# A selective-scan block on one core: three shared PSUM banks for products, one Silu for four chunks, decays computed ahead in SBUF, and B times u for two states in one instruction

## What is computed

```
xn = layer_norm(x); xs, z = split(xn @ in_w)            # 512 channels each
xc = silu(causal_conv4(xs) + conv_b)
delta = softplus(xc @ xd_w @ dtp_w + dtp_b)
Bm = xc @ xB_w;  Cm = xc @ xC_w                         # 16 states each
dA = exp(delta * A);  dBx = (delta * xc) * Bm
h_t = dA_t * h_(t-1) + dBx_t;   y_t = sum over n of h_t * C_t      # for each of 16 states
out = ((y + D * xc) * silu(z)) @ out_w + x
```

## Time and profile before

| what | us |
|---|---|
| median of 3 runs | 11806.0 |
| lowest and highest | 11800.15, 11808.89 |
| the profiled execution | 11784.14 |
| its span, first to last instruction | 11782.3 |
| busy: TensorE, VectorE, ScalarE, GpSimd | 9023.3, 9032.0, 5977.4, 7664.1 |
| mean granted TensorE clock | 0.829 |

### The profile page before, as it was taken

How to read it: one execution, slowest core, us unless ns; L and a number is a source line. 1 busy time by engine, 2 the same in 40 slices (tenths; PEclk the granted TensorE clock), 3 DMA queues, 4 the chain that set the end, 5 groups by cost and what they waited for, 6 DMA issues and landing times. The chain is left out here.

```text
span 11782.3 us, 151965 instructions
## 1 busy us (share of the span) xinstructions
PE 9023.3 (77%) x42776; PEld 7086.5 (60%) x42776; DVE 9032.0 (77%) x13553; ACT 5977.4 (51%) x8945; POOL 7664.1 (65%) x7270
## 2 busy tenths in 40 slices
PE   6777777777777777777777777777777777799998
PEld 5656555555556555655565555556565655577776
DVE  5888888888888888888888888888888888333332
ACT  4555555555555555555555555555555555244443
POOL 5777777777777777777777777777777778100000
PEclk7878787888888788888788878888888787799999
DMA  2221122222211222222211222122211221000000
GB/s 80 76 68 63 63 78 72 76 70 71 76 65 57 73 78 72 78 68 76 71 64 58 78 72 78 68 71 76 68 64 62 78 72 66 22 11 11 11 11 9
DMA packets 366106, 730.08 MB, mean 62 GB/s; under 512 B 143670, under 2 KB 188890, under 8 KB 365274
## 3 DMA queue, kind: packets, MB, share of 16 engines
q1 hardware_dynamic: 361560, 717.54, 18.3%
q10 hardware_dynamic: 3714, 2.89, 0.1%
HBM read 699.27 MB, written 21.05 MB: 61 GB/s over the span
## 5 line engine op out<-in xcount | busy, mean ns | idle before, releaser
L443 POOL TENSOR_TENSOR bu<-b_all,u_buf 128x514 f32<-128x514 f32 x4096 | 5100.3, 1269 | 156.6 <-DVE ch L837 150.9
L654 ACT ACTIVATE decay<-delta,neg_a 128x512 f32<-128x512 f32 x4096 | 2805.9, 689 | 3436.8 <-DVE h_ps L837 2248.6
L1080 PE MATMUL y_ps<-ident,ch 128*128 128x128 f32 x16384 | 2940.2, 322 | 1747.3 <-DVE ch L855 851.4
L1080 PEld LDWEIGHTS y_ps<-ident,ch 128*128 128x128 f32 x16384 | 2193.9, 164 | 2571.3 <-DVE ch L855 1339.9
L837 DVE TENSOR_TENSOR_SCAN ch<-decay,bu 128x256 f32<-128x256 f32 x4096 | 2908.6, 730 | 778.1 <-ACT decay L654 766.3
L837 DVE TENSOR_TENSOR_SCAN h_ps<-decay,bu 128x256 f32<-128x256 f32 x4096 | 2836.4, 736 | 273.2 <-POOL bu L443 120.3
L452 POOL TENSOR_TENSOR ch<-ch,c_all 128x512 f32<-128x512 f32 x1024 | 1345.5, 1314 | 1974.1 <-DVE ch L837 1973.6
L966 PE MATMUL w_ps<-xn,in_w 128*128 128x257 f32 x4096 | 1235.3, 457 | 280.6 <-ACT xn L559 151.6
L855 DVE TENSOR_TENSOR ch<-h_ps,c_all 128x512 f32<-128x512 f32 x2048 | 1357.4, 663 | 42.6 <-issue 42.6
L855 DVE TENSOR_TENSOR ch<-ch,c_all 128x512 f32<-128x512 f32 x1024 | 1213.5, 1185 | 0.0
L966 PEld LDWEIGHTS w_ps<-xn,in_w 128*128 128x128 f32 x4096 | 920.9, 235 | 472.7 <-issue 158.3
(11 more groups left out here) (247 smaller groups left out, 11126.1 us busy)
## 6 DMA issues: line engine op xcount, KB each, us to landing
b_all<-bc_dram SPq DMA_DIRECT2D x512, 514.0 KB, 4.2
c_all<-bc_dram SPq DMA_DIRECT2D x512, 514.0 KB, 5.8
in_w<-in_L_attn_in_w SPq DMA_DIRECT2D x64, 1024.0 KB, 5.0
x_in<-in_x SPq DMA_DIRECT2D x128, 256.0 KB, 2.6
out_w<-in_L_attn_out_w SPq DMA_DIRECT2D x64, 512.0 KB, 3.9
h_mid<-h_cur SPq DMA_DIRECT2D x32, 257.0 KB, 2.2
h_F<-h_mid SPq DMA_DIRECT2D x16, 514.0 KB, 3.6
out<-o_sb SPq DMA_DIRECT2D x64, 86.0 KB
```

What stands on the lines that cost most here:

```text
L443: pool.tensor_tensor(bu[:, s % NBU, :, :].rearrange("p b s -> p (b s)"), b_all[:, n // NU, n % NU, :, :].rearrange("p b s -> p (b s)"), u_ ...
L654: func(decay[:, s % NDP, :].rearrange("p (b t) -> p b t", b=NB), delta[:, c, :, 1:S], ACT.Exp, scale=neg_a[:, k, c, n:n + 1]).then_inc(dec ...
L1080: last = pe.matmul(y_ps[:, k, :], ch[:, s % NPR, k * P:(k + 1) * P], ident[:, :], is_transpose=True, start=False, stop=(n == NST - 1 and k ...
```

## The change

- **PSUM.** `w_ps` becomes one tensor of three banks. A product on an even place uses banks 0 and 1, one on an odd place banks 2 and 1, so two products in a row share bank 1. The wait for a free bank is now made for each image (`bank_free`, `read_earlier`): the second image's bank waits until the product just before has been read. The y products now take one bank instead of two. The bank that this frees goes to `h_ps`, which now has two buffers.
- **h.** Every state whose C times h is made on VectorE has its h in PSUM; only the states of `POOL_C` still have it in SBUF.
- **Silu.** Gates and convolution outputs are evicted with Identity, one chunk in a unit. One Silu over all four chunks (2056 columns) in SBUF follows, in unit 9 (12 for the fourth job) for the gates and in unit 23 or 24 for the convolution. Four table loads a job instead of eight. New semaphores `gates_ready` and `xc_ready` tell of the two; `output`, `first_tokens`, `delta_x` and the projections wait for them.
- **Decays ahead.** In front of each Silu three decays (NDS = 3) are computed ahead into `early_decay`, in SBUF: for a Silu in unit u the states 2u + 4 to 2u + 6. The scans of these states read their decay there.
- **B times u.** One instruction makes both states of a unit (1028 columns), with u broadcast over the two. It waits until both states two units back are scanned, and the scans wait for it as one.
- **Places.** y0 is made in unit 11 instead of 9 (15 instead of 12 in the fourth job), `token_rows` stands at the end of a unit, and the centred inputs, the convolution and the step sizes are spread anew.

The core of the diff:

```diff
-NBU, NPR, NDP = 4, 8, 2
+NBU, NPR, NDP, NDS = 4, 8, 2, 3
...
     def y_at(jj):
-        return (12 if jj == 4 else 9), 18, (26 if jj in (2, 4) else 25)
+        return (15 if jj == 4 else 11), 18, (26 if jj in (2, 4) else 25)
+
+    def silu_at(jj):
+
+        return gates_at(jj) + 4, conv_at(jj) + 9
+
+    def early(jj):
+
+        return [NU * u + NDP + 2 + i for u in silu_at(jj) for i in range(NDS)]
...
+    def read_earlier(name, g, jj, b):
+
+        i = slot(name, g, jj)
+        last = i - 2
+        if b == 1 and i > 0 and bank_count((final_key_at if is_final(g) else key_at)[i - 1][0]) == NB:
+            last = i - 1
+        return None if last < 0 else (last % 2, g * (n_body // 2) + (last // 2 + 1))
...
-        h_ps = ctx.enter_context(nc.psum_tensor("h_ps", [P, NB * L], F32))
+        h_ps = ctx.enter_context(nc.psum_tensor("h_ps", [P, NU, NB * L], F32))
         decay = ctx.enter_context(nc.psum_tensor("decay", [P, NDP, NB * L], F32))
-        w_ps = [ctx.enter_context(nc.psum_tensor(f"w_ps{i}", [P, NB, BANK], F32)) for i in range(2)]
+        w_ps = ctx.enter_context(nc.psum_tensor("w_ps", [P, 3, BANK], F32))
...
-            return w_ps[slot(name, g, jj) % 2]
+            odd = slot(name, g, jj) % 2
+            if bank_count(name) == 1:
+                return w_ps[:, 2 * odd, :]
+            return w_ps[:, 2:0:-1, :] if odd else w_ps[:, 0:2, :]
+
+        def decay_slot(jj, s):
+
+            if s in early(jj):
+                return early_decay[:, early(jj).index(s) % NDS, :]
+            return decay[:, (s - len([v for v in early(jj) if v < s])) % NDP, :]
...
+                if positive(job_count(g, jj, STATES, NU * u - NU)):
+
+                    pool.wait_ge(scan_done, job_count(g, jj, STATES, NU * u - NU))
+                at = NU * (u % (NBU // NU))
+                pool.tensor_tensor(bu[:, at:at + NU, :, :].rearrange("p n b s -> p n (b s)"),
+                                   b_all[:, n, :, :, :].rearrange("p n b s -> p n (b s)"),
+                                   u_buf[:, c % 2, :, :].rearrange("p b s -> p (b s)").unsqueeze(1).to_broadcast([P, NU, T]),
+                                   ALU.mult).then_inc(b_done, 1)
...
-                func(xc[:, jj % 2, c, :, :], w[:, :, 0:S], ACT.Silu, bias=conv_b[:, k, c:c + 1]).then_inc(read_of(f"cv{c}", g, jj), 1)
+                func(xc[:, jj % 2, c, :, :], w[:, :, 0:S], ACT.Identity, bias=conv_b[:, k, c:c + 1]).then_inc(read_of(f"cv{c}", g, jj), 1)
+
+            def conv_silu(g, jj):
+
+                for c in (2, 3):
+                    act.wait_ge(read_of(f"cv{c}", g, jj), nth(f"cv{c}", g, jj))
+                func(xc[:, jj % 2, :, :, :], xc[:, jj % 2, :, :, :], ACT.Silu).then_inc(xc_ready, 1)
+                act.preload_act_table_set(LOG_EXP)
...
+                    if u in silu_at(jj):
+                        for i in range(NDS):
+                            decays(g, jj, NU * u + NDP + 2 + i)
...
             def scan(g, jj, s, b):
-                inside = s % NU == 0
+                inside = s not in POOL_C
...
-                h = h_ps[:, :] if inside else ch[:, s % NPR, :]
+                h = h_ps[:, s % NU, :] if inside else ch[:, s % NPR, :]
                 cols = slice(b * L, (b + 1) * L)
-                last = dve.tensor_tensor_scan(h[:, cols], decay[:, s % NDP, cols], bu[:, s % NBU, b, 1:],
+                last = dve.tensor_tensor_scan(h[:, cols], decay_slot(jj, s)[:, cols], bu[:, s % NBU, b, 1:],
                                               bu[:, s % NBU, b, 0:1], ALU.mult, ALU.add)
```

More of the change, by code:

```diff
@@ L62, in later_keys @@
     def later_keys(jj, keys):
-        for name, before in [("y2", "dt0"), ("y1", "cv1" if jj in (2, 4) else "xs2")] + [("y0", "cen0" if jj == 4 else "var")]:
+        for name, before in [("y2", "dt0"), ("y1", "cv1" if jj in (2, 4) else "xs2")] + [("y0", "t0"), ("y0", "xs0")]:
             at = [i for i, key in enumerate(keys) if key[0] == before]
+            if name == "y0" and ((name, jj) in keys or before == "t0" and not at):
+                continue
             keys = keys[:at[0]] + [(name, jj)] + keys[at[0]:] if at else [(name, jj)] + keys
@@ L255, in banks, with decay_user @@
         def banks(name, g, jj):
-            return w_ps[slot(name, g, jj) % 2]
+            odd = slot(name, g, jj) % 2
[6 more added lines that the diff above has]
+            return decay[:, (s - len([v for v in early(jj) if v < s])) % NDP, :]
+        def decay_user(jj, s):
+            if s in early(jj):
+                return s - 2 * NDS
+            plain = [v for v in range(STATES) if v not in early(jj)]
+            k = plain.index(s)
+            return plain[k - NDP] if k >= NDP else k - NDP
         def full_of(name, g, jj):
@@ L905, in period @@
                         size = g, jj, u
-                    elif u in (29, 30) and not last:
-                        size = g, jj + 1, u - 29
+                    elif u - conv_at(jj) in (15, 16) and not last:
+                        size = g, jj + 1, u - conv_at(jj) - 15
                     s = NU * u
@@ L1007, in centre @@
                     sources = ("o0", jj - 2), ("o1", jj - 2)
-                for j in range(CM):
+                for j in part:
                     product(f"cen{j}", g, jj, lambda b: [(minus_centre[:, :] if c == j else mean_w[:, :], x[:, c, b, :])
```

186 lines of the change are left out of this document (103 added, 83 removed).

## The result

| what | us |
|---|---|
| changed kernel, median of 4 runs | 11729.8 (11727.7 to 11729.9) |
| kernel before, median of 4 runs beside them | 11803.1 (11790.9 to 11808.9) |
| ratio | 0.9939, 95% interval 0.9922 to 0.9956 |
| span of the profiled execution, before and after | 11782.3, 11728.1 |

A forecast was written before the change was run, and what follows sets the result against it. VectorE was taken as the bound, GpSimd close behind. Terms -535 - 636 + 250 + 0 + 350 + 100 = -471; 11784 - 471 + 22 = 11335 us, range 10800 to 11850 us.

The forecast's parts named there:

- C times h out of PSUM, -535: On VectorE, 1024 products C times h go from 1185 to 663 ns, all booked as time: -535 us.
- three banks bind TensorE: Rival: evictions hold TensorE, so VectorE waits for y or a product buffer, 4 us a job: 11591 us, chance 0.14.
- Decay waits, -636: VectorE's 848.5 us of waits for decays: a quarter stays, -636 us; ends -424 and -848.
- The turns: Scans with decay in SBUF alternate with GpSimd's instructions: 3.9 us a job in the second group (states 50 to 52), +250 us.
- the multiply pair of the earlier trace: Evidence for turns: two VectorE multiplies with SBUF inputs took 2.75 us, where 680 ns is the shortest of one.
- The slower rival: Every early scan waits for a whole GpSimd instruction, at 1.7 us each: 704 us more, 12039 us, chance 0.18.
- y wait and first group, 0: VectorE's 350.8 us wait for y booked against turns of early scans in states 22 to 24: 0, with 300 either side.
- Pair product: On GpSimd, one B times u instruction for two states takes 2.25 us, bounds 2.05 and 2.54.
- its gating: B times u for even units starts late, so GpSimd's other work delays VectorE: +350 us, bounds +100 and +700.
- Other two-input work, +100: VectorE's other two-input instructions wait longer for longer GpSimd instructions: +100 us.
- A long y_added wait: Sign that the prediction is wrong: a long wait for TensorE's y_added, of which the trace before has none.

The follow-up runs named there:

- places of y: Changed kernel with y0 asked for in unit 13 instead of 11 (not in the fourth job) and y2 in unit 28: 11525.2 us, ratio 0.9762.
- the best version: Changed kernel without decays ahead, B times u one state at a time, y0 and y2 later, y copied out before the convolution's Silu block: 10902.3 us, ratio 0.9246.

## Why the prediction was wrong in its size

Point by point, in its own order.

- **C times h out of PSUM, -535.** The duration was right (663 forecast, 673 measured). The whole of it was booked as time, and that was not: it was paid for with a shared bank, 248 us, and the rest mostly became waiting for y and for B times u. The prediction had the bank's price as its rival "three banks bind TensorE", at +256 and chance 0.14, and as an either-or. It was true, and no rival to the others but one of the terms: eight product buffers did not hide it. That 248 meets 256 so closely is in part luck: of the waits that the rival names, for y and for a product buffer, the bank makes 133 us.
- **Decay waits, -636.** Measured -592: 256 us stayed where 212 were forecast. The decays ahead account for 371 of it; without them 221 us are gone too (848.5 to 627.5). The step on which it rests, that five states in hand cover the block, holds. Of the 256 us, 193 lie in two waits of 7.66 and 5.20 us that come back in 15 of the 16 groups, and in those at 1854 and 2058 us ScalarE itself stands for TensorE, as the prediction said of what stays.
- **The turns.** They exist, as the multiply pair of the earlier trace rows said; 1226 ns a scan where about 1.5 us were forecast, since behind y GpSimd had run dry: with the y wait gone the mean is 1438. The Trainium skill (SBUF — State Buffer, Who interferes with whom) says that a VectorE instruction with two SBUF inputs contends with a GpSimd one that reads SBUF. The run with all decays in SBUF agrees for scans: 736 ns become 1271. The slower rival, a whole GpSimd instruction for each scan, did not come true: GpSimd waits for scans itself (2047 us for C times h, 535 for the pair), as the prediction said against it.
- **y wait and first group, 0: the step that failed.** For what it describes, y0, the booking came out: y0's wait fell by 145 us and the first group's turns cost about as much, half of 333. But it booked the whole 350.8 us of y wait by y0 alone and put y1 and y2 at nothing, without a reason. They had not waited before, and now wait 69 and 397 us. The convolution's block stands ahead of y2 as the gates' block stands ahead of y0, y2 is asked for in the same unit as before, and two things come on top: the y copy moved behind the block (145 us by itself), and the projections, once 8 matmuls in each of two units, now one piece of 16. Asked for in unit 28, y2 is never waited for. Forecast -351 for the y wait, measured +321.
- **Pair product.** 2.23 us an instruction where 2.25 was taken; its gating +246 for +350. The mechanism held, down to what it rests on: two short instructions with one signal cost the same.
- **Other two-input work, +100.** +74, but not evenly: L894 and L899 got slower, while the multiply of the earlier trace rows went from 1340 to 684 ns. It still meets GpSimd, but is first now, behind a wait for y in which GpSimd had run dry, and GpSimd is the one that is held, 2.23 us where 1.27 is usual:

```profile
4676.05 1.28 DVE L885 TENSOR_TENSOR cen<-cen,rstd 128x514 f32<-128x514 f32 x2
4676.21 2.23 POOL L500 TENSOR_TENSOR ch<-ch,c_all 128x512 f32<-128x512 f32 x1 [6.69 <-DVE ch L915]
```

- **A long y_added wait** was named as a sign against: 42 us, small, and probably in the trace of before as well, as the idle of 42.6 us before C times h.

The parts were also not independent. By single undoing they cost 369 (decays ahead), 306 (pair), 209 (places of y) and 145 (y copy), 1029 together, and 818 in one kernel. The decays ahead removed 371 us of decay waits (627.5 to 256) and yet cost 369 us. A wait for decays is not time saved when it goes: 363 us of it came up again as waits for y.

What stays open: how much of the y wait belongs to each of decays ahead, bank and block. Undone one at a time the decays ahead take away 363 us, moving the copy 139, the shared bank 95 (with h in SBUF); these need not add. The block itself, one Silu over four chunks, was never undone, and without decays ahead y2 still waits 210 us. For the 69 us at y1 no run shows a cause.

## What to carry to other kernels

When one engine's long block makes another wait, do not ask only whether its next customer is covered; list everything behind the block on that engine and who stands behind each, and do it for every block, above all for those where nothing waits so far: here the y that had all of the wait was looked at, and the one that had none got it. A buffer that costs the bounding engine anything (here 0.5 us a scan) must beat the wait it removes after that wait has moved on. And fusing two instructions on an engine that wasn't the bound saved no time here, but halved how finely its buffers turn over: with four buffers and one signal for two, that cost 306 us.

## What the runs showed of the hardware

- A tensor_tensor_scan with both inputs in SBUF takes turns with GpSimd's instructions: 736 ns becomes 1271 in the mean, and GpSimd's product 1210 becomes 1468.
- Behind the two stalls looked at, TensorE ran at the lower clock for some us, which makes a stall cost more than its length. 33 times (131.7 us together) TensorE stands for the convolution's Silu before the 16 matmuls of the projections, in the first window below for 3.99 us. The two windows of the changed kernel hold these 16 matmuls there and in the job shown above:

```profile
4724.60:4731.10 6.50, 6.50 (x17) 3.44 (x17) 5.09 (x5) 1.84 (x2) 5.22 (x5) 0.55 0.00 0
4885.50:4890.10 4.60, 4.60 (x18) 2.55 (x17) 0.00 (x0) 0.00 (x0) 0.77 (x1) 0.79 0.00 0
```

  At a granted 0.55, so mostly at the lower level of 1.2 GHz, they take 6.5 us, at 0.79 4.6. The granted clock was 1.00 in the 5 us before the first stall, 0.50 in the 3.4 us behind it, 0.61 in the next 3.1 and 1.00 then. In the second place TensorE had stood 8.31 us before the y matmuls; these took the stretch at 0.50 (3.7 us), and the projections came behind them. Over the whole run the mean of these matmuls is 506 ns where it was 387 before the change. The mean clock of the whole run is 0.821 in the changed kernel and 0.862 in the best version, in which TensorE's waits for VectorE's products (541.9 to 380.7 us) and for the y copy (247.1 to 58.9) are shorter.
